# Four graph layers on one core: the one-hot comparison reads its node numbers from a PSUM bank

## Time and profile before

| | us |
|---|---|
| median of 3 runs | 8074.86 |
| lowest and highest | 8072.14, 8080.34 |
| profiled execution, its own time | 8083.27 |
| its span in the profile | 8081.4 |

### The profile page before, as it was taken

The page is one execution under the profiler, slowest core; times in us unless marked ns, Lnnn a source line. Parts: engine busy times, 40 slices in busy tenths (PEclk is TensorE's granted clock), DMA queues, the critical chain, the costliest instruction groups (busy, mean ns, idle before and its releaser), DMA issues. The chain is left out here.

```text
span 8081.4 us, 86320 instructions
## 1 busy us (share of the span) xinstructions
PE 4591.5 (57%) x20103; PEld 3072.2 (38%) x20222; DVE 4954.4 (61%) x18680; ACT 1892.6 (23%) x4901; POOL 5452.5 (67%) x5731
## 2 busy tenths in 40 slices
PE   3343452444443444459788888878884566433343
PEld 3333332444433444434333333333334556333333
DVE  4333362444453444477688888888888998533334
ACT  0000031222222222231023323222235665400001
POOL 7777717777737777712277777777765777577775
PEclk6555565555565555579899999999998999655555
DMA  2111113333322333338899999999986887111111
GB/s 73 51 51 51 51 25 83 78 78 77 77 61 71 77 79 78 74 134 336 307 347 348 349 349 346 345 348 344 346 311 222 281 279 253 35 51 51 51 51 52
DMA packets 572435, 1348.04 MB, mean 167 GB/s; under 512 B 101141, under 2 KB 138997, under 8 KB 558761
## 3 DMA queue, kind: packets, MB, share of 16 engines
q0 software_dynamic: 228864, 628.13, 26.0%
q1 hardware_dynamic: 328604, 689.76, 24.1%
q10 hardware_dynamic: 14476, 24.62, 1.0%
HBM read 1003.21 MB, written 338.89 MB: 166 GB/s over the span
## 5 line engine op out<-in xcount | busy, mean ns | idle before, releaser
L942 POOL DMA_INDIRECT gat_ring<-gat_table,psrc_idx x1664 | 1643.5, 988 | 777.3 <-issue 498.2
L578 DVE TENSOR_TENSOR acc<-acc,bank 128x129 f32 (+1 forms) x1664 | 480.2, 289 | 1250.1 <-PE bank L541 1205.4
L1931 POOL DMA_INDIRECT pair<-right_table,idx_r_idx x782 | 788.5, 1008 | 365.8 <-issue 212.8
L510 POOL DMA_INDIRECT gcn_sum_ring<-gcn_table,src_idx x782 | 769.8, 984 | 275.2 <-issue 238.0
L1931 POOL DMA_INDIRECT acc<-left_table,idx_l_idx x782 | 789.9, 1010 | 238.7 <-issue 208.1
L510 POOL DMA_INDIRECT gin_sum_ring<-in_x,src_idx x782 | 781.2, 999 | 250.7 <-issue 237.1
L2006 ACT ACTIVATE positive<-positive 128x512 f32<-128x512 f32 x782 | 492.2, 630 | 1588.9 <-DVE positive L2036 1588.9
L1984 PE MATMUL bank<-pair,ident 128*128 128x512 f32 x1564 | 832.7, 615 | 1.3 <-issue 0.7
L1006 PE MATMUL bank<-gat_ring,gat_hot 128*128 128x130 f32 x3328 | 719.8, 392 | 118.1 <-DVE gat_hot L1126 116.1
L541 PE MATMUL bank<-gcn_sum_ring,gcn_sum_hot 128*128 x1664 | 417.8, 431 | 619.1 <-DMA gcn_sum_ring<-gcn_table,src_idx 586.4
L541 PE MATMUL bank<-gin_sum_ring,gin_sum_hot 128*128 x1664 | 405.2, 420 | 569.7 <-DMA gin_sum_ring<-in_x,src_idx 534.2
(11 more groups left out here) (521 smaller groups left out, 8770.9 us busy)
## 6 DMA issues: line engine op xcount, KB each, us to landing
kept<-acc SPq DMA_DIRECT2D x391, 512.0 KB, 6.1
x_rows<-kept SPq DMA_DIRECT2D x195, 1024.0 KB, 5.3
gat_place<-local_rows SPq DMA_DIRECT2D x128, 416.0 KB, 3.9
left_table<-rel_out SPq DMA_DIRECT2D x49, 1032.0 KB, 5.0
right_table<-rel_out SPq DMA_DIRECT2D x49, 1032.0 KB, 3.9
feat<-attr_rows SPq DMA_DIRECT2D x194, 256.0 KB, 7.9
gat_ring<-gat_table,psrc_idx POOLq DMA_INDIRECT x1664
types<-type_rows SPq DMA_DIRECT2D x98, 256.0 KB, 6.1
```

What stands on the lines that cost most here:

```text
L510: e.indirect_dma_start(ring[:, at:at + F], None, table[:, :], bass.IndirectOffsetOnAxis(ap=ed["src"][:, i:i + 1], axis=0)).then_inc(*got[b ...
L942: e.indirect_dma_start(ring[:, at:at + TROW], None, table[:, :], bass.IndirectOffsetOnAxis(ap=ed["psrc"][:, i:i + 1], axis=0)).then_inc(*g ...
L1931: e.indirect_dma_start(to[j % NG][:, n * LROW:(n + 1) * LROW], None, tab[:, :], bass.IndirectOffsetOnAxis(ap=idx[:, i:i + 1], axis=0)).the ...
```

## The change

The plain sums copy `node_iota` into columns 0 to 127 of bank 6 once, ahead of the loop, wait for the copy, and compare from there. The attention layers do the same with bank 4, and to have it free their products of lots take turns in two pairs of banks (0 to 3) instead of three. In the attention layers the copy stands behind the clearing of `acc` and is waited for with it. `begin("carried")` makes the semaphore for the plain sums' copy. Nothing is changed in the relational layer, whose comparisons (L2095) are made by POOL from SBUF.

```diff
@@ aggregate_rows
         sums = lambda b, n: k.psum[2 * (b % NP2) + n // 2][:, n % 2 * 256:n % 2 * 256 + width]
+        iota = k.psum[2 * NP2][:, 0:P]
+        iota_laid, = k.begin("carried")
         if plan:
             plan.begin()
...
                 if plan:
                     e.wait_ge(*plan.dve.now())
+                e.tensor_copy(iota, c["node_iota"][:, :]).then_inc(*iota_laid.up())
+                e.wait_ge(*iota_laid.at(1))
                 def make(b, made):
                     e.tensor_tensor(
                         hot_of(b)[:, :].rearrange("p (t n) -> p t n", n=P),
-                        c["node_iota"][:, :].unsqueeze(1).to_broadcast([P, Q, P]),
+                        iota.unsqueeze(1).to_broadcast([P, Q, P]),
                         over(ed["local"][:, b * Q:(b + 1) * Q], P), ALU.is_equal).then_inc(*made.up())
@@ gat_edges
-        NH, NP2, U = 3, 3, CT // GR
+        NH, NP2, U = 3, 2, CT // GR
...
         bank_d, bank_t = k.psum[6], k.psum[7]
+        iota = k.psum[2 * NP2][:, 0:P]
...
                             e.tensor_tensor(
                                 hot[i % NH][:, :].rearrange("p (t n) -> p t n", n=P),
-                                c["node_iota"][:, :].unsqueeze(1).to_broadcast([P, HQ, P]),
+                                iota.unsqueeze(1).to_broadcast([P, HQ, P]),
                                 over(ed["local"][:, i * HQ:(i + 1) * HQ], P), ALU.is_equal).then_inc(*hot_made.up())
...
                 for t, v in ((acc, 0.0), (step, -BIG), (met, -BIG), (rest, -BIG)):
                     e.memset(t[:, :], v).then_inc(*zeroed.up())
+                e.tensor_copy(iota, c["node_iota"][:, :]).then_inc(*zeroed.up())
                 e.wait_ge(*zeroed.now())
```

## The result

The changed kernel takes **7967.85 us** (median of 4 runs, 7959.53 to 7968.54) against 8074.21 for the kernel before on the same chip (4 runs, 8072.14 to 8080.34): a ratio of 0.9868, with a 95% interval of 0.9855 to 0.9882, or 106.4 us less. The prediction said 7963. The profiled execution took 7967.27 us (span 7965.1), 116.0 less than the one shown of before.

A forecast was written before the change was run, and what follows sets the result against it. POOL issuing 3,228 gathers back to back was taken to pace three stages. Savings of 31.3, 33.8 and 46.6 us sum to 111.7; off the profiled 8083.27 that gives 7971.6, less 8.4 to the median, 7963 us; range 7945 to 7990.

The forecast's parts named there:

- A comparison holds the gather that starts under it, and a bank operand frees it: Plain sums and attention layers: moving one comparison input from SBUF to a bank removes the comparisons' whole hold, 111.7 us.
- first rival: Nothing is released, the hold coming from the comparison's length or 512-column write: 8075 to 8077 us, chance 0.05.
- When a gather is held: A gather reads something about 0.14 us after its start; a comparison then running keeps it out until it ends.
- The sum: Time held by comparisons over both plain sums and the attention layers, taken from means less medians: 111.7 us.
- Last sum: Plain sum of layer 3: (984 - 944) ns x 782 gathers, 31.3 us, all of it from comparisons.
- First sum: Plain sum of layer 0: 36.8 us of stretching, less 3.0 under the planner's VectorE work, leaves 33.8 us.
- Attention layers: Two attention layers: 59.9 us of stretching, less 13.3 not due to comparisons, leaves 46.6 us.
- One for one on the path: The 111.7 us shortens the three gather-paced stages one for one; each ends with its last gather plus an unchanged tail.
- The new comparison costs nothing: Closing tails, 44 comparisons: about 683 ns from the bank, cost 0; 2.8 us by the skill's cycle counts.
- third rival: Slow bank read of four repeats: comparisons of 2.74 us in tails and inner chunks, 8200 us, chance 0.02.
- Copies and four banks cost nothing: Four copies with waits stay covered, cost 0 (1.6 us uncovered); the four-bank wait ends before the comparison's, cost 0.
- second rival: The four banks bind in the attention layers' closing chunks: 21 us over 26 lots, 7984 us, chance 0.03.

The follow-up runs named there:

- plain_only: Only the plain sums' part of the change, against the kernel before: 7996.03 us, ratio 0.9925, 63.2 us less.
- gat_only: Only the attention layers' part of the change, with their copies and four banks, against the kernel before: 8017.86 us, ratio 0.9949, 41.4 us less.
- local_in_bank: Kernel before, but plain sums' comparisons read the edges' node numbers from banks 6 and 7, node_iota staying in SBUF: 8002.07 us, ratio 0.9929.
- all_but_read: The changed kernel with copies, waits and four banks kept, but both comparisons reading SBUF again: 8059.68 us, ratio 0.9996 against the kernel before.
- mask_in_place: Changed kernel with the relational layer's 2048-column product cut into four 512-column pieces, left back to back: 7947.21 us, 16.4 under the changed kernel rerun.

## Why the prediction was right, step by step

- **A comparison holds the gather that starts under it, and a bank operand frees it.** Right, and shown: plain_only, gat_only and local_in_bank gain, all_but_read doesn't. The first rival, that nothing is released, is out. The passage of the Trainium skill named beside it ("SBUF — State Buffer", Who interferes with whom) infers that a tensor_tensor leaves descriptor generation alone. What the prediction drew from that, nothing to win, is contradicted with 106.4 us. The inference itself isn't: the same section says that a VectorE instruction with two SBUF inputs contends with a GpSimd instruction that reads SBUF. A gather takes its row numbers from SBUF (`src_idx`). That the comparison acts on a gather's early point alone would fit both, but no run tells the reading of the row numbers from the making of descriptors.
- **When a gather is held.** Too simple in the prediction. It says that a gather asks about 0.14 us after its start and that a comparison then running keeps it out. By that, a gather begun shortly ahead of a comparison would be held too. In the plain sums of the kernel before, 42 gathers begin up to 0.125 us ahead of one, and none is held. A timeline of the kernel before:

```profile
7118.67 0.94 POOL L510 DMA_INDIRECT gcn_sum_ring<-gcn_table,src_idx  x1 [0.31 <-issue]
7118.76 0.68 DVE L557 TENSOR_TENSOR gcn_sum_hot<-node_iota,e_local 128x512 f32<-128x512 f32 x1
```

So the held ones are those that begin under a comparison, but not in its last 0.13 us. The sum doesn't change, since it was taken from means and medians.
- **The sizes.** Last sum: 31.3 predicted, 30.6 less busy. First sum: 33.8 and 33.8; its mean came to 956 ns, the top of what was foretold, with 11 gathers still held, 3.0 us in all, as allowed. Attention layers: 46.6 predicted, 44.3 measured, at 961 ns. The step that is 2.3 too high is the share left to spreads and scans: 13.3 was allowed, and (961 - 952) ns x 1,664 = 15.0 us is left. That freed gathers come to stand under a spread instead is likely but not shown: gathers begun under a spread were 20, held for 5.5 us, in the kernel before, and are 29 for 6.6 us after.
- **One for one on the path.** Right. (The prediction's "no more than 27 short stops" of POOL leaves out the waits ahead of a stage's first gather, 12.7 us in the first sum, which are 12.5 after.) The first gather of the attention layers starts 36.3 us sooner than in the earlier trace rows, the last 80.4, the first of the last sum 85.6, its last 116.3. Of these steps 36.3, 44.1 and 30.7 belong to the changed stages and 5.2 to the relational layer, whose code is the same in both.
- **The sum.** 111.7 predicted; 108.7 in the gathers, 106.4 between the medians, 116.0 between the profiled executions. The last holds 5.2 from the relational layer and 2.4 from the stretch between the first sum and the attention layers, in code that is the same (108.7 + 5.2 + 2.4 = 116.3, the difference of the spans); the profiled execution of before lay 8.4 over the median of the three runs that the prediction had, that of after within 0.6 of its own. That the prediction's 111.7 from the median and the 106.4 measured differ by 5.3 is no more than the runs of one kernel scatter (8 to 9 us).
- **The new comparison costs nothing.** Right: 680 to 684 ns on the mean against 684 to 686. The 120 and 58 cycles of the Trainium skill ("VectorE: DVE Perf Modes", the TRN2 errata) don't show in this form. In the 128-column tensor_scalar a difference does show, 342 against 302 ns. The 62 cycles would be 65 ns, an estimate from that page; 40 were measured, and no run tells how much of the 40 is a fixed cost. The third rival, at 8200, is out.
- **Copies and four banks cost nothing.** Right: all_but_read stands at 0.9996, and TensorE never waits for the additions of the attention layers (L1142). The second rival, at 7984, is out.

## What to carry to other kernels

When a queue of gathers paces a stage, compare the mean of its issues with their median: a gap of a few per cent is time to win, and the timeline shows whose instructions lie over the starts of the long ones, or begin shortly after them and end just ahead of them. Move one input of such an instruction to a bank where one is free; where none is, cut a long SBUF-only instruction into pieces with other work between them; here that paid (33.4 us) though the pieces together took 44.5 us longer on VectorE, which was not what paced the stage. Rate it by the mean above the median times the number of gathers, since the undisturbed gather stays as it is.

## What was not expected of the hardware

- The hold does not chain: with the comparison made twice, each held gather waited for one instruction only, and the kernel took 44.7 us more in place of the 185 to 235 expected.
- Back-to-back pieces are not always separate: 14 gathers of mask_in_place waited past the end of the piece under which they began, and 15 that began 0.03 to 0.05 us ahead of the fourth piece were held by it. Open.
- A tensor_scalar with a single SBUF input holds gathers too, 0.65 us of spread as fully as a comparison, and it also holds those that began 0.21 to 0.46 us ahead of it. Which property of an instruction decides, beyond "an input in a bank frees it" for the forms tried here, is open: no run put a spread's input in a bank.
- The same comparisons held gathers for less in a later profile: all_but_read shows 992 and 979 ns where the earlier trace rows shows 999 and 984. They are about as many (191 against 190), but held for 56.0 us in all and not 66.1. gat_only, whose plain sums are those of before, shows the same (992 and 978). The kernel before, too, ran 15 us faster there. Whether this comes from the chip or from the run is open.
